# Cross-attention scores with turned keys and four 32-row strips in a post-norm decoder layer, and a new merge order

## The reference

```python
x = layernorm(x + self_attention(x))     # causal, 16 heads of 128, 2 key/value heads, rotary, tanh cap 30
x = layernorm(x + cross_attention(x))    # below
x = layernorm(x + ffn(x))                # router picks 4 of 16 blocks of 64, gelu, 1024 hidden

# cross attention: 16 heads of D = 16 over a context of 256 rows
q = w8a8_linear(x, wq, bq)               # rows and weights rounded to 8-bit integers, then scaled
k = cond @ wk.T + bk ;  v = cond @ wv.T + bv
scores = einsum('bhnd,bhld->bhnl', q, k) / sqrt(D) + mask[:, None]
o = einsum('bhnl,bhld->bhnd', softmax(scores), v)
return w8a8_linear(o, wo, bo)            # the rows of o are rounded too
```

## Time and profile before

| | us |
|---|---|
| median of 3 executions | 382.76 (382.37 to 385.27) |
| span of the profiled execution, first to last instruction | 382.7 |
| PE busy | 370.5, 97% |
| DVE busy | 293.5, 77% |
| ACT busy | 233.6, 61% |
| POOL busy | 151.0, 39% |

### The profile page before, as it was taken

How to read it: one execution, slowest core, us unless ns; L and a number is a source line. 1 busy time by engine, 2 the same in 40 slices (tenths; PEclk the granted TensorE clock), 3 DMA queues, 4 the chain that set the end, 5 groups by cost and what they waited for, 6 DMA issues and landing times.

```text
span 382.7 us, 8976 instructions
## 1 busy us (share of the span) xinstructions
PE 370.5 (97%) x3038; PEld 315.8 (82%) x3038; DVE 293.5 (77%) x900; ACT 233.6 (61%) x494; POOL 151.0 (39%) x172
## 2 busy tenths in 40 slices
PE   8999999999999999999999999999999998999894
PEld 7678897978889888787998787989887897778783
DVE  2999888865688487899888868887878888976443
ACT  1658655545576865465686863867794455995240
POOL 4697947457544414454432332441302530000111
PEclk9999999999999999999999999999999999999999
DMA  8991753653524243124344221121121200000000
GB/s 283 367 345 57 249 174 75 189 169 84 166 84 109 88 137 113 46 75 155 111 109 140 57 57 40 47 82 57 45 82 48 79 2 2 15 16 2 0 30 27
DMA packets 21404, 38.42 MB, mean 100 GB/s; under 512 B 2544, under 2 KB 12144, under 8 KB 21360
## 3 DMA queue, kind: packets, MB, share of 16 engines
q1 hardware_dynamic: 20544, 37.06, 31.4%
q10 hardware_dynamic: 816, 0.79, 0.6%
HBM read 25.52 MB, written 5.24 MB: 80 GB/s over the span
## 4 chain that ended last, share of the span: by engine, by line
PE 80%; DVE 10%; issue 3%; DMA 3%; POOL 2%; ACT 1%; SPq 0%; POOLq 0%; DVEq 0%; ACTq 0%
PE acc L595 10%; PE bank L489 10%; PE bank L680 8%; PE bank L562 6%; PE bank L741 6%; PE bank L761 6%; PE bank L539 5%; PE bank L692 4%; PE bank L669 3%; PE bank L565 3%; PE bank L576 3%; PE bank L547 3%; PE bank L621 2%; PE bank L658 2%; PE bank L508 2%
## 5 line engine op out<-in xcount | busy, mean ns | idle before, releaser
L918 ACT ACTIVATE xs<-xs,xneg 128x256 f32<-128x256 f32 x128 | 53.5, 499 | 13.2 <-DVE xneg L1197 13.2
L1362 POOL TENSOR_TENSOR q_T<-q_T,rope_s 128x512 f32<-128x512 f32 x24 | 31.7, 1323 | 63.1 <-DMA rope_s<-rope_t 58.0
L1373 POOL TENSOR_TENSOR a_lo<-a_flat,a_hi 128x512 fp32r<-128x512 f32 x32 | 42.7, 1336 | 22.6 <-ACT a_flat L838 22.6
L595 PE MATMUL acc<-wo_s,a_hi 128*128 128x256 f32 x256 | 50.6, 296 | 0.0
L1197 DVE CUSTOM_DVE_ANT_0 xs<-bank,mask_s 128x256 f32<-128x256 f32 x128 | 45.7, 419 | 5.0 <-PE bank L669 4.6
L1391 POOL TENSOR_TENSOR small<-small,half 128x1 f32<-128x1 f32 x24 | 13.9, 584 | 75.9 <-DVE small L1081 75.9
L562 PE MATMUL bank<-v_s,p_near 128*128 128x129 f32 x256 | 42.0, 277 | 0.9 <-POOL p_near L1380 0.6
L595 PEld LDWEIGHTS acc<-wo_s,a_hi 128*128 128x128 f32 x256 | 39.4, 189 | 2.6 <-issue 2.6
L562 PEld LDWEIGHTS bank<-v_s,p_near 128*128 128x128 f32 x256 | 35.4, 191 | 5.1 <-issue 3.8
L489 PE MATMUL bank<-x_hi,wqkv_hi 128*128 128x256 f32 x124 | 38.6, 311 | 0.0
L595 PE MATMUL acc<-wo_s,a_lo 128*128 128x256 f32 x128 | 35.9, 280 | 0.0
(11 more groups left out here) (168 smaller groups left out, 970.1 us busy)
## 6 DMA issues: line engine op xcount, KB each, us to landing
wo_s<-wo_parts SPq DMA_DIRECT2D x24, 512.0 KB, 3.3
rope_s<-rope_t SPq DMA_DIRECT2D x54, 128.0 KB, 2.3
wo_parts<-wo_s SPq DMA_DIRECT2D x8, 512.0 KB, 3.3
xs<-in_wo SPq DMA_DIRECT2D x8, 256.0 KB, 5.8
stage<-in_wqkv SPq DMA_DIRECT2D x2, 512.0 KB, 5.1
xp_T<-in_wqkv SPq DMA_DIRECT2D x2, 512.0 KB, 6.9
y<-in_x SPq DMA_DIRECT2D x4, 256.0 KB, 3.1
ctx_s<-in_ctxT SPq DMA_DIRECT2D x4, 256.0 KB, 3.1
```

What stands on the lines that cost most here:

```text
L595: ins = mm(acc[:, t, :], a[x], wo_s[:, slot, w, m, :], start=(j == 0 and t == 0 and m == 0 and p == 0), stop=(j == PAIRS - 1 and m == 1 an ...
L918: activation(xs[:, t, m, m2, :], xs[:, t, m, m2, :], ACT.Exp, bias=xneg[:, t, m, m2:m2 + 1], scale=-1.0)\
L1362: g.tensor_tensor(dst, dst, (rope_s if b else rope_t)[:, n % 2], ALU.add).then_inc(sig["rotated", 0], 1)
L1373: g.tensor_tensor(a_lo[:, j % 2], a_flat[:, j % 2], a_hi[:, j % 2].bitcast(F32), ALU.subtract)\
```

## The change

Keys are made already turned, by making the weight the stationary operand: features lie on the partitions (`context_keys`), one product for 128 features = 8 heads. Values stay as they were, in a bank of their own. A strip of 32 partitions holds two heads. `kM` holds, for each of the two heads (e = 0, 1), the strip's keys with the other head's rows set to zero (multiplied by a 0/1 column `half_s`), as hi (ACT) and lo (DVE, `rest_keys`, a new list entry `rest_k`). The queries are turned once per token tile, plain float32, two transposes (`turn_q`); ACT writes hi and DVE lo. `xscore(b, c, t)`, c = 0, 1, now serves 8 heads: four row strips of 32, each into a bank of its own, 512 columns (two heads x 256), and three products one after another in each strip (hi·hi, hi·lo, lo·hi). Mask and exponentials become entries of their own, `soft(b, i, t)`, one per bank, and `xs` has four slots for a tile instead of two. `load_context` of the next batch waits for `rest_keys` instead of the context product, since the keys overwrite `ctx_s`. A DMA of 128 x 4 numbers (`cols_s`) is added at the start. `ORDER` is another string, 575 letters instead of 563.

```diff
 def context_ops(b):
-    return [*prep, *(("ctx", b, t, 0) for t in range(TT)), *(("turn_k", b, g, 0) for g in range(QUADS))]
+    return [*prep, *((kind, b, 0, 0) for kind in ("ctx_k", "ctx_v", "rest_k"))]
 def cross_ops(b, t):
-    ops = [("quant_x", 0), ("turn_x", 0), ("query", 0), ("turn_q", 0), ("xscore", 0), ("turn_q", 1)]
-    for g in range(QUADS):
-        ops += [("turn_p", 2 * g), ("turn_p", 2 * g + 1)]
-        if g + 1 < QUADS:
-            ops.append(("xscore", g + 1))
-        if g + 2 < QUADS:
-            ops.append(("turn_q", g + 2))
-        ops.append(("xmix", g))
+    ops = [("quant_x", 0), ("turn_x", 0), ("query", 0), ("turn_q", 0)]
+    for c in range(CK):
+        ops += [("xscore", c), *(("soft", c * XHALF + r) for r in range(XHALF))]
+        for i in range(c * XHALF, (c + 1) * XHALF):
+            ops.append(("turn_p", i))
+            if i % 2:
+                ops.append(("xmix", i // 2))
...
 ORDER = (
-    "rrrmrrsmrmssrmrrsrmmmmrsssmmrmrmssmmmmmrrmmmmmmrmmmsssmcmmrrccmmmrmmcmcccmcccmmmssrrmccsmmmcmmmrsmxmmmssr"
+    "rrrrrrrmrmsssmrrsmsmmrmsmmsmsrmrsmrmmmmsmmmcmsmccmmmmsmmrrmmmmmmmmmmmrmrccrrmmmmrmcmxmsccscscsxysrmmcxmsm"
...
@@ PE
+            def context_keys(b):
+                ps = claim("ctx_k", b)
...
+                for c in range(CK):
+                    for k in range(CK):
+                        ins = mm(ps[:, c * T:(c + 1) * T], wkv_s[:, k, c * P:(c + 1) * P], ctx_s[:, k, :],
+                                 start=(k == 0), stop=(k == CK - 1))
...
+            def xscore(b, c, t):
+                ps = [claim("xscore", b, c, t, r) for r in range(XHALF)]
+                wait_for(pe, "k_lo", b, 1)
+                wait_for(pe, "q_lo", b, 0, t)
+                for q, k in ((0, 0), (0, 1), (1, 0)):
+                    for r in range(XHALF):
+                        tile = slice(XROWS * r, XROWS * (r + 1))
+                        ins = mm(ps[r][:, :], qT[tile, t, q, c, :], kM[tile, k, c].rearrange("p e n -> p (e n)"),
+                                 start=(q == k), stop=(q == 1))
...
-                for m2 in range(2):
-                    for m in range(2):
-                        r = slice(64 * m, 64 * m + 64)
-                        ins = mm(ps[m][:, m2 * T:(m2 + 1) * T], qS[r, t, g % 2, m2, :], kS[r, g, m2, :], start=True, stop=True)
@@ ACT
+            def context_keys(b):
...
+                for e in range(2):
+                    nc.scalar.mul(kM[:, 0, :, e], kf[:], half_s[:, e:e + 1]).then_inc(sig["k_hi", 0], 1)
@@ DVE
+            def context_keys(b):
...
+                v.tensor_tensor(kf[:], bank("ctx_k", b)[:].rearrange("p (c n) -> p c n", c=CK),
+                                bk_s.unsqueeze(2).to_broadcast([P, CK, T]), ALU.add).then_inc(sig["kf", 0], 1)
...
+            def rest_keys(b):
...
+                for e in range(2):
+                    wait_for(dve, "k_hi", b, e)
+                    v.scalar_tensor_tensor(kM[:, 1, :, e], kf[:], half_s[:, e:e + 1], kM[:, 0, :, e].bitcast(F32),
+                                           ALU.mult, ALU.subtract).then_inc(sig["k_lo", 0], 1)
...
+            def turn_q(b, t):
...
+                v.tensor_tensor(qT[:, t, 1].rearrange("p c q -> p (c q)"), bank("turn_q", b, 0, t)[:, 0:CK * P],
+                                qT[:, t, 0].bitcast(F32).rearrange("p c q -> p (c q)"), ALU.subtract).then_inc(sig["q_lo", t], 1)
```

More of the change, by code:

```diff
@@ L47 @@
 XPAIRS = XH // 2
+XHALF = XPAIRS // 2
+XROWS = 2 * XD
 XW = 2 * XD
@@ L460, in _ @@
                     load_tokens(b + 2)
-                elif kind == "ctx" and i == TT - 1 and b + 1 < B:
+                elif kind == "rest_k" and b + 1 < B:
                     load_context(b + 1)
-                elif kind == "xscore" and i == QUADS - 1 and both and b + 1 < B:
+                elif kind == "soft" and i == XPAIRS - 1 and both and b + 1 < B:
                     load_mask(b + 1)
@@ new lines, in turn_q, with soft @@
+            def turn_q(b, t):
+                wait_filled(dve, "xscore", b - 1, 1, t, XHALF - 1)
+                wait_for(dve, "q_hi", b, 0, t)
+                v.tensor_tensor(qT[:, t, 1].rearrange("p c q -> p (c q)"), bank("turn_q", b, 0, t)[:, 0:CK * P],
+                                qT[:, t, 0].bitcast(F32).rearrange("p c q -> p (c q)"), ALU.subtract).then_inc(sig["q_lo", t], 1)
+            def soft(b, i, t):
+                do, _ = steps(sig["xmasked", t], b * PER_TILE["xmasked"] + 2 * i)
+                if i == 0:
+                    dve.wait_ge(mask_in, 16 * (b + 1))
+                n = b * XPAIRS + i
+                slot = n % XHALF
+                if n >= XHALF:
+                    was_b, was_i = divmod(n - XHALF, XPAIRS)
+                    wait_filled(dve, "turn_p", was_b, was_i, t)
+                c, r = divmod(i, XHALF)
+                wait_filled(dve, "xscore", b, c, t, r)
+                for e in range(2):
+                    do(v.tensor_tensor_reduce(out=xs[:, t, slot, e, :], in0=bank("xscore", b, c, t, r)[:, e * T:(e + 1) * T],
+                                              in1=mask_s[:, t, :], scale=-1.0, scalar=3.0e38, op0=ALU.add,
+                                              op1=ALU.min, accum_out=xneg[:, t, slot, e:e + 1]))
@@ L1305, in _ @@
                     turn_w(i)
-                elif kind == "ctx":
-                    context(b, i)
+                elif kind == "ctx_v":
+                    context_keys(b)
+                    context_values(b)
+                elif kind == "rest_k":
+                    rest_keys(b)
                 elif kind == "quant_x":
@@ L1427 @@
     cos, sin = rope_tables()
+    halves = (np.arange(P)[:, None] // XD % 2 == np.arange(2)).astype(np.float32)
     arrays = {
```

203 lines of the change are left out of this document (90 added, 113 removed).

## The result

The changed kernel is slower: 390.67 us median (388.46 to 391.95, four executions) against 382.92 (382.37 to 385.27, four) on the same chip, ratio 1.0166, 95% interval 1.0113 to 1.0219. The forecast was 373.0, with a range that ended at 381.0.

A forecast was written before the change was run, and what follows sets the result against it. PE was taken as the bound up to 305 us, with PE, DVE and ACT nearly level in a later 30 us stretch. 382.7 - 12.2 + 1.6 + 1.0 = 373.1, say 373 us, range 367.5 to 381.

The forecast's parts named there:

- What bounds the kernel: PE bounds it up to 305.2 us, idle 3.6 us; in a later 30 us stretch PE, DVE and ACT are nearly level.
- What goes: Key and query transposes: 112 fewer at 0.109 us each, 12.2 us less PE, counted in full where PE is the bound.
- the scores: Cross scores: 16 visits of three steps replace 32 of four products, 15.2 us against 13.6, 1.6 dearer (1.3 to 2.4).
- the entry: Cross-score visits: PE's extra cost of entering a visit from other work, 0.09 us each.
- The two rivals about strips: Cross scores: four strips partly hinder each other (376 us, chance 0.08) or take turns two and two (383.7 us, 0.05).
- The rest of the order: Everything else moves a little; at the start PE waits at most half a microsecond less for POOL; 0 (-2 to +8).
- VectorE as cover: Off PE's path, DVE and ACT each lose about 13 us; nothing booked, useful only as cover for new waits.
- The last stretch: Last cross attention: PE waits about 2 us for DVE's keys and queries, against shorter DVE and ACT work; +1.0 (-1.5 to +4).
- Slower by the claims: Cross-score visits take four of seven banks and PE waits for DVE's masks; 389 us at 1.0 us a visit; chance 0.06.
- the two signs that the prediction named for being wrong: Four strips not running at once, or PE's waits for banks adding up to more than 5 us before 295.
- The base: Starting time of the sum: the profiled execution's 382.7 us, taken to be the median too.

The follow-up runs named there:

- map_new: The changed kernel's instructions in the order of the kernel before, each step standing where the one it replaces stood; 448.1 us.
- lite_new: The changed kernel with three GpSimd additions and subtractions cut to an eighth of their columns or less, the rest left out; 377.57 us, ratio to the kernel before 0.9826.
- pad_new: lite_new with three fills of an unread buffer ahead of each shortened GpSimd operation, so GpSimd is busy but hardly reads SBUF; 382.99 us.
- relaid_old2: The kernel before's instructions in a new order: strip products together, few table loads, no long waits, VectorE's SBUF work off GpSimd's; 389.19 us, ratio 1.0123.

## Why the prediction was wrong

**What bounds the kernel.** Right for the path, wrong in what followed from it. "PE stands idle 3.6 us in all" up to 305 us was read as nothing to win there. It was also the sign that this order had no slack to give: 3.6 us of waiting in 305 is what a laid-out order buys, and a new one has to buy it again.

**What goes** (-12.2) **and the scores** (+1.6). Right. A visit was forecast at 0.86 alone and measured 0.90, a step at 0.22 (the third round starts 0.23 after the second), the entry at 0.09 and measured 0.09. Busy TensorE was to be near 361 and is 361.3; the sum itself gives 359.9, 1.4 less. (The lower end of the scores' +1.6 comes to 1.4, not 1.3.) The two rivals about strips, with 13% of the chances, are refuted. The Trainium skill's speedup of 3.07 for four row tiles (page "TensorE: Matmul & The Clock Gate", section "Measured speedup vs the span model") gave an estimate of 0.29 us a step, 1.07 a visit with the 0.20 beyond its steps; the measured 0.23 and 0.90 decide against that estimate. The page's factor itself, which may hold the first load and the run-out, is not put to the test here.

**The rest of the order, "I take 0, between -2 and +8".** This step failed. It measured +10: the last piece of the output projection began at 305.1 us, not at 295. 6.3 of them are the order's in the first 75 us, by the two kernels with crossed first parts. I had asked there only whether PE waits less for POOL's rotary sums, and took VectorE at its mean durations from the earlier trace rows. Nothing in the sum asked what VectorE's instructions would run beside. Of the 13.2 us by which TensorE's idle time grew in the whole program, 8.4 are waits for VectorE and 2.9 for GpSimd. With GpSimd's load cut the changed kernel gains 13.1 us and the one before 2.7; about half of the gain (5.3 of 10.8 by spans, 7.7 of 13.1 by medians) is not GpSimd's own lateness. In the first 100 us this cut leaves TensorE idle 1.8 us of 9.6, and 5.3 when GpSimd's time is given back. So what costs is where the new order has put two things: the roundings, next to GpSimd's reads, and GpSimd's results, close to their use. That these two make up all of the +10 is not shown.

**VectorE as cover.** "About 13 us less each" for DVE and ACT was to be spare. ACT's busy time fell by 9.1 (233.6 to 224.5). DVE's fell by 5.3 (293.5 to 288.2): with GpSimd's columns cut in both kernels it differs by 11.8 (284.2 to 272.4), so 6.5 us of the missing are the collisions, and some of them stand in a chain for which TensorE waits.

**The last stretch** (+1.0, up to +4). Behind that piece the program takes 81.6 us, against 77.5 before: +4.1, just past the upper bound. The wait that was forecast at 2 us is there (`L676 <- DVE qT`, 1.0 of its 1.3 us are in this stretch), but idle time in the stretch grew by 3.5 us (8.6 to 12.1), most of it in many small waits.

**Slower by the claims** (0.06, 389 us). The number came near by luck, the mechanism didn't come: claims cost 0.6 us in the changed kernel. In `map_new` they cost 41. The changed order had spread the softmax steps well and paid in other places. Neither of the two signs that the prediction named for being wrong came: the strips ran at once, and before 295 us no wait for a bank that the masks held shows. The failure was not on its list.

**The base.** The time outside the span is 1.75 us in every execution, so "the profiled execution's 382.7 us, which is the median too" compared a span with times. And a clock of 0.983 to 0.987 in three executions puts the median 2.2 us above the profiled one. The sum of the miss: busy 1.4, idle 12.2, outside the span 1.75, other executions 2.2, together 17.6 of 17.7 us. The profiled execution of the kernel before was itself above its median (382.7 + 1.75 = 384.5 against 382.9), so the two kernels differ by 4.0 us in span and by 7.8 in median.

What stays open: how much of the 5.4 us between `lite_new` and `pad_new` is due to GpSimd's writes; why the rules of `relaid_old2`, which gave the new instructions 10 us, made the old ones 5 us slower (its trace shows VectorE busy 306.3 us, 12.8 more than before, with the group of `L1106` and `y` at a mean of 548 ns where it had 368, so the rules did not keep the roundings clear of GpSimd there); and whether a still better order would bring the new instructions their full 10 us.

## What to carry to other kernels

When a change comes with a new order, price the order as a change of its own: idle time of the bound engine that is near zero is an asset of the old order, and "the rest moves a little" puts it all at risk. For every VectorE operation in a chain that the bound engine waits for, look at what GpSimd runs beside it. And before trusting a re-laid order, count groups of strip products, table loads, and waits of two or three microseconds.

## What the runs showed of the hardware

- VectorE's SBUF-to-SBUF multiplication of 256 columns that begins a rounding took 0.35 us alone and 1.36 to 1.48 us beside a GpSimd subtraction of 1.3 us; cutting GpSimd's columns took 15.8 us off VectorE's busy time with its own program unchanged.
- A step followed by products in strips cost TensorE 0.09 us more, one that follows them 0.06 more (0.53 and 0.50 against 0.44 for the same four transposes).
- Four 32-row strips of 512 columns, three rounds, took 0.90 us. The second round started 0.34 us after the first and the third 0.23 after the second, and the four products of a round within 0.01 us: nearly full overlap.
- TensorE's granted clock was 0.51 to 0.55 in the 5 us behind stretches in which it had 1.7 to 2.8 us of work in five, and stayed at 1.00 behind a single wait of 2.67 us in one execution, while three others of that kernel had a mean of 0.983 to 0.987.
- A change between the exponential and the hidden layer's function on ScalarE cost a load of 1.28 us each way.
